# Lightning attention layer: values for four heads in 512-column matmuls, half of them passed through memory

## The chip, the cores and the metric

One core of one Trainium2 chip runs the whole kernel. The metric is the device time in microseconds (us) of one execution, median of three runs. Engines are named as in the profile: PE is the matrix engine (TensorE), PEld its weight loads, DVE the vector engine, ACT the scalar engine, POOL the GpSimd engine, SP the engine whose queue issues most transfers. A difference is stated as time after minus time before.

## The reference, cut to what matters

A decoder layer: attention over x, then a small cross attention, then a feed-forward block with 8-bit rounding. The change touches only the first part:

```python
qkv = silu(einsum('bnf,of->bno', layernorm(x), w_qkv))      # 16 heads, 128 wide, 512 inputs
q, k, v = split(qkv)                                        # per head
# per block of 64 rows: o = (q*q_decay) @ kv + (q @ k.T * diag_decay) @ v ; kv = block_decay*kv + (k*k_decay).T @ v
out = norm_w * out * rsqrt(mean(out*out) + eps)             # over all heads of a row
x = x + (sigmoid(layernorm(x) @ w_gate.T) * out) @ w_out.T
```

The input has 8 sequences of 512 rows; the kernel computes the recurrence of each head as one causal product with weights exp(-slope * distance) over the 512 rows.

## The kernel before

**Tiling.** The 16 heads are 8 pairs (p = 0 to 7). For each pair the kernel goes through the 8 sequences (b), and for each sequence through the two heads of the pair (j). One such step is a *slot*, n = 0 to 127, with v = n // 2 the number of the (pair, sequence). Every product is made of three passes over values split in a high and a low part (fp32r), listed in PASSES, so a product over 512 inputs is 4 chunks times 3 passes, 12 matmuls for a destination.

**PE in one slot**, in this order (lines of the kernel before): the scores of head n, 12 matmuls of 512, 384, 256 and 128 columns (L828); queries and keys of head n + 1, 24 matmuls of 512 columns, and the gate of head n, 12 more (all L746, `head_rows`); the output product of head n, 12 matmuls of 512 to 128 columns (L867); then half of the values of the next sequence for both heads of the pair, `values` (L755): 2 row tiles times 12 matmuls of 256 columns. In seven early slots (PREPARED) PE also transposes the normed x of a further sequence; in p = 7 it sums squares.

**DVE in one slot**: four products scores times decay, called sf (L1037 to L1041); the half of the values (product with the sigmoid, high part, low part: L890, L892, L894); the low part of the decayed scores, sl (L1049, three pieces); the same three steps for the queries and for the keys of n + 1, ending in kl; then extra work of some slots; then, when the output product is there, the gated head og (L1079), its high part (L1086) and its low part (L1088). **ACT** makes the sigmoids of values, queries, keys and gate (L614, L602, L608, L691), the high part of the scores, sh (L668), and the squares of the output, sq (L707). **POOL** adds the squares (L553), makes the low parts of weights (L453) and masks feed-forward rows (L504).

**Extra work.** From slot 29 on, feed-forward weights are prepared, one tile for every three slots: 22 tiles of 512 columns and, for the steps in slots 96 to 107, four of 1408 columns. In slots 30, 33, 36 and so on DVE finds the row scale (L979 to L986) before og, and ACT scales the rows (L621, L622) after sq. In the slots after these DVE rounds (L991, L996) before og, and ACT's queue issues a transpose (L628) after sq. ACT's sigmoid of the values comes behind these in its queue.

**Transfers.** SP loads x (2 MB, high and low, two buffers) after the gate of the second head, stores the gated heads of a sequence (1 MB, two buffers `og_out`) after og of the second head, and loads weights of the next pair, 4 times 512 KB, at the start of a pair. Everything is ordered by the loops over `slots()` and by semaphores written out by hand: an engine works off its list in order and stops at a wait.

## Time and profile before

| | |
|---|---|
| median of 3 runs | 2636.26 us (2635.76 to 2637.02) |
| profiled execution, whole | 2635.24 us |
| its span (first to last instruction) | 2633.5 us |
| PE / DVE / ACT / POOL busy | 2592.7 / 2103.1 / 1087.0 / 704.4 us |
| attention part | up to 1944.88 us, 128 slots |
| moved by transfers | 372.06 MB, mean 141 GB/s |

How to read a row of the timeline: start and length in us, engine, line, operation, destination <- sources, shape, count; in square brackets how long the engine was idle before and what ended that. The row of a matmul is longer than its distance to the next one, because matmuls overlap: what a matmul costs is the distance from start to start. The sum of 1.74 us (2635.24 less 2633.5) around the span is taken as unchanged.

### The profile page before, as it was taken

To read this page: it belongs to the slowest core of one execution; us is meant where nothing else is said; L and a number is where in the kernel's file an instruction comes from. 1 tells how busy PE (TensorE), PEld (TensorE's weight loads), DVE (VectorE), ACT (ScalarE), POOL (GpSimd) and SP (SyncE) were. 2 spreads that over 40 slices of the span, in tenths; PEclk is the share of its full clock that TensorE was granted. 3 is DMA by queue.
4 is the path that set the end of the run, shared out by engine and by line. 5 is a ranking of instruction groups with operands and counts; after the bars stand their busy time and mean duration, and the time that the engine had idled before them with its cause. 6 is when DMAs were issued, how large, how long until landed. Compare 5 with 4: busy or idle time off the path is not lost. (4 is left out here: it accounts for less than half of the span.)

```text
span 2633.5 us, 40074 instructions
## 1 busy us (share of the span) xinstructions
PE 2592.7 (98%) x14271; PEld 2174.6 (83%) x14271; DVE 2103.1 (80%) x3870; ACT 1087.0 (41%) x1848; POOL 704.4 (27%) x1034
## 2 busy tenths in 40 slices
PE   9999999999999999999999999999989999999995
PEld 8888888888888888888888888888877676767762
DVE  8887887877787788778777988776657888888887
ACT  5444322433343343334334343433224555555553
POOL 3112101311131131114111321311123444444444
PEclk9999999999999999999999999999999999999998
DMA  6653323343353334434344634342256556556642
GB/s 224 241 192 128 129 98 130 117 141 111 110 167 126 106 111 149 146 105 144 105 135 130 160 124 127 135 172 97 96 207 197 158 153 171 151 162 168 163 109 56
DMA packets 200917, 372.06 MB, mean 141 GB/s; under 512 B 97168, under 2 KB 100112, under 8 KB 192016
## 3 DMA queue, kind: packets, MB, share of 16 engines
q1 hardware_dynamic: 117024, 340.78, 38.9%
q10 hardware_dynamic: 81360, 20.07, 4.4%
q0 software_dynamic: 2336, 8.65, 1.0%
q8 instruction: 115, 1.88, 0.3%
q14 instruction: 82, 0.67, 0.1%
HBM read 252.80 MB, written 96.61 MB: 133 GB/s over the span
## 5 line engine op out<-in xcount | busy, mean ns | idle before, releaser
L746 PE MATMUL bank<-attention_xT,attention_w_hi 128*128 128x512 f32 x3064 | 952.0, 392 | 0.5 <-DVE attention_shared L947 0.5
L746 PEld LDWEIGHTS bank<-attention_xT,attention_w_hi 128*128 128x128 f32 x3064 | 566.0, 188 | 111.2 <-issue 0.6
L746 PE MATMUL bank<-attention_xT,attention_w_lo 128*128 128x512 f32 x1532 | 597.2, 390 | 0.0
L553 POOL TENSOR_TENSOR attention_sq_sum<-attention_sq_sum,attention_sq 128x512 f32<-128x512 f32 x120 | 192.1, 1601 | 1058.9 <-ACT attention_sq L707 1058.7
L755 PE MATMUL bank<-attention_w_hi,attention_xT 128*128 128x256 f32 x2048 | 379.7, 286 | 1.0 <-DMA attention_xT<-normed_turned 0.8
L746 PEld LDWEIGHTS bank<-attention_xT,attention_w_lo 128*128 128x128 f32 x1532 | 287.5, 188 | 61.7
L755 PEld LDWEIGHTS bank<-attention_w_hi,attention_xT 128*128 128x128 f32 x2048 | 317.9, 192 | 1.7 <-issue 1.7
L1037 DVE TENSOR_TENSOR attention_sf<-bank,attention_dcy 128x512 f32<-128x512 f32 (+1 forms) x256 | 147.6, 618 | 178.9 <-PE bank L828 178.7
L755 PE MATMUL bank<-attention_w_lo,attention_xT 128*128 128x256 f32 x1024 | 289.5, 283 | 0.0
L1431 PE MATMUL bank<-finish_w_out_hi,finish_og 128*128 128x512 f32 x824 | 282.4, 407 | 0.2
L668 ACT CAST attention_sh<-attention_sf 128x384 fp32r<-128x384 f32 (+1 forms) x384 | 185.4, 547 | 121.3 <-DVE attention_sf L1037 121.3
L1049 DVE TENSOR_TENSOR attention_sl<-attention_sf,attention_sh 128x384 fp32r<-128x384 f32 (+1 forms) x384 | 226.7, 645 | 0.0
L1259 POOL TENSOR_TENSOR finish_t<-finish_silu,finish_u 128x512 f32<-128x512 f32 (+1 forms) x96 | 120.3, 1253 | 309.8 <-ACT finish_silu L1329 309.8
L755 PEld LDWEIGHTS bank<-attention_w_lo,attention_xT 128*128 128x128 f32 x1024 | 196.0, 191 | 0.0
L1079 DVE SCALAR_TENSOR_TENSOR attention_og<-bank,attention_nw,attention_gate 128x512 f32<-128x512 f32 x128 | 95.9, 749 | 118.5 <-PE bank L867 118.4
L707 ACT ACTIVATE attention_sq<-bank 128x512 f32<-128x512 f32 x128 | 76.6, 599 | 273.7 <-DVE attention_og L1079 273.7
L1431 PEld LDWEIGHTS bank<-finish_w_out_hi,finish_og 128*128 128x128 f32 x824 | 154.8, 188 | 37.9 <-issue 0.4
L691 ACT ACTIVATE attention_gate<-bank 128x512 f32<-128x512 f32 x128 | 76.6, 598 | 255.4 <-PE bank L746 255.4
L608 ACT ACTIVATE attention_sig_k<-bank 128x512 f32<-128x512 f32 x128 | 76.6, 599 | 244.5 <-PE bank L746 244.5
L828 PE MATMUL bank<-attention_ql,attention_kh 128*128 128x512 f32 (+3 forms) x512 | 165.2, 323 | 0.0
L867 PE MATMUL bank<-attention_sh,attention_vl 128*128 128x512 f32 (+3 forms) x512 | 165.1, 322 | 0.0
L867 PE MATMUL bank<-attention_sl,attention_vh 128*128 128x512 f32 (+3 forms) x512 | 164.6, 321 | 0.0
(218 smaller groups left out, 4942.8 us busy)
## 6 DMA issues: line engine op xcount, KB each, us to landing
attention_xT<-normed_turned SPq DMA_DIRECT2D x62, 2048.0 KB, 8.7
gated_heads<-attention_og_out SPq DMA_DIRECT2D x64, 1024.0 KB, 7.9
finish_og<-gated_heads SPq DMA_DIRECT2D x103, 512.0 KB, 3.9
finish_og_last<-gated_heads SPq DMA_DIRECT2D x25, 512.0 KB, 4.0
normed_turned<-attention_shared SPq DMA_DIRECT2D x24, 512.0 KB, 3.9
attention_shared<-in_w_head SPq DMA_DIRECT2D x16, 512.0 KB, 8.2
finish_x<-in_x SPq DMA_DIRECT2D x32, 256.0 KB, 4.2
out<-finish_x SPq DMA_DIRECT2D x32, 256.0 KB, 4.2
```

Of the source, the lines that this page charges most:

```text
L553: g.tensor_tensor(sq_sum[:, col_b], sq_sum[:, col_b], sq[:, :], ALU.add).then_inc(s_acc, 1)
L608: nc.scalar.activation(sig_k[:, :], K_BANK[:, :], ACT.Sigmoid).then_inc(s_sigk, 1)
L668: nc.scalar.copy(sh[:, a:e], sf[:, a:e]).then_inc(s_sh, 1)
L746: mm = pe.matmul(dst[:, :], part[a][w][:, k, col:col + P], xT[i][:, b, k, :], start=(k == 0 and s == 0), stop=(k == KD - 1 and s == 2))
L755: mm = pe.matmul(bank_[:, t * 2 * P:(t + 1) * 2 * P], xT[i][:, b, k, (2 * j + t) * P:(2 * j + t + 1) * P], part[a][V_W][:, k, :], start=(k ...
L828: mm = pe.matmul(dst, (kh, kl)[a][:, t * P:(t + 1) * P], (qh, ql)[e][:, Q0[t]:S], start=(s == 0), stop=(s == 2))
L867: mm = pe.matmul(O_BANK[:, Q0[t]:S], (vh, vl)[a][i][:, t, j * P:(j + 1) * P], (sh, sl)[e][:, OFF[t]:OFF[t + 1]], start=(t == 0 and s == 0) ...
L1037: v_.tensor_tensor(sf[:, OFF[k]:OFF[k + 1]], S_BANK[k][:, 0:S - Q0[k]], d[:, 0:S - Q0[k]], ALU.mult).then_inc(s_sf, 1)
L1049: v_.tensor_tensor(sl[:, a:e], sf[:, a:e], sh[:, a:e].bitcast(F32), ALU.subtract).then_inc(s_sl, 1)
L1079: v_.scalar_tensor_tensor(out=og[:, :], in0=O_BANK[:, :], scalar=nw[:, 2 * p + j:2 * p + j + 1], in1=gate[:, :], op0=ALU.mult, op1=ALU.mul ...
L1259: g.tensor_tensor(t_[:, a:a + w], sg[k % 2][:, 0:w], u_[k % 2][:, 0:w], ALU.mult).then_inc(s_t, 1)
L1431: mm = pe.matmul(Y_BANK[:, :], og[Q % RING][:, j, a, :], wo[b][:, q * HQ + j, :], start=(q == 0 and j == 0 and s == 0), stop=(q == 3 and j ...
```

## The change

Only every other pair (even p) makes values now, for four heads at once: for one row tile, 12 matmuls of 512 columns (two pairs times two heads times 128). Such a block is called a *quad*; a sequence has four. The half for the own pair goes to the value tiles; the half for the next pair goes to a small tile `held`, is stored to memory (256 KB a quad) and is loaded again (1 MB a sequence) one pair later. `begun_in(n)` tells which two quads belong to slot n: the first is made at the end of slot n, where `values` stood, the second in slot n + 1 between the scores and the queries. Slots with v + 1 in an odd pair have none. There is one bank for both, so the second quad waits until DVE has multiplied the first by its sigmoid (semaphore `v_steps`), and DVE and ACT take the first quad at the head of slot n + 1, the second one behind sl. Before slot 0 there are three quads in place of two halves.

To make room, `og_out` and the decay table have one buffer each; the value weights (512 columns) are in one tile, refreshed in the third and seventh sequence of odd pairs; the exponentials of the decay table are made one at a time, and the triangle mask covers only 128 columns. Two more pieces of the output weights are converted ahead of slot 126.

The diff, cut to its core:

```diff
-        wh[w], wl[w] = sb(f"w_hi{w}", [P, RAW], F32R), sb(f"w_lo{w}", [P, RAW], F32R)
+    wv = [sb(f"w_{l}{V_W}", [P, KD, 4 * P], F32R) for l in ("hi", "lo")]
+    held = [sb(f"held{i}", [P, 2, 2 * P], F32R) for i in range(2)]
-    og_out[1] = sb("og_out1", [P, KT, 2, 2, P])
+    og_out = sb("og_out", [P, KT, 2, 2, P])
+    def begun_in(n):
+        v = n // 2 + 1
+        p, b = v // B, v % B
+        return None if v >= NP * B or p % 2 else KT * (p // 2 * B + b) + 2 * (n % 2)
-    SPLIT = {LAST - 13: 0, LAST - 11: 1, LAST - 9: 2, LAST - 7: 3}
+    SPLIT = {LAST - 13 + 2 * q: q for q in range(6)}
...
+            if begun_in(n - 1) is not None:
+                for q in range(2):
+                    store_values(begun_in(n - 1) + q)
+            if j == 0 and v + 1 < NP * B and (v + 1) // B % 2:
+                sp.wait_ge(s_o, n)
+                load_values((v + 1) // B, (v + 1) % B, 1 - v % 2)
...
+        values_lo(0)
+        values_lo(1)
...
         for n, v, p, b, j in slots():
-            if n < LAST:
-                sig_values(n + 1)
+            q = begun_in(n - 1)
+            if q is not None:
+                sig_values(q)
...
                 nc.scalar.copy(sh[:, a:e], sf[:, a:e]).then_inc(s_sh, 1)
+            if q is not None:
+                sig_values(q + 1)
...
+        def values(q):
+            if q > 1:
+                pe.wait_ge(s_vm, 2 * (q - 2) + 3 if q > 2 else 1)
+            for k in range(KD):
+                for s, (a, b) in enumerate(PASSES):
+                    mm = pe.matmul(v_bank(q)[:, :], xT[i][:, b, k, t * P:(t + 1) * P], wv[a][:, k, :],
+                                   start=(k == 0 and s == 0), stop=(k == KD - 1 and s == 2))
+            mm.then_inc(s_v, 1)
...
-        values(0, 0)
-        values(1, 0, v_bank(1))
+        for q in range(3):
+            values(q)
...
+            if begun_in(n - 1) is not None:
+                values(begun_in(n - 1) + 1)
             if not last:
...
-                pe.wait_ge(s_vl, n + 2)
-                values(j, 1 - i)
+            if begun_in(n) is not None:
+                wait_x(v + 1)
+                values(begun_in(n))
...
+        def values(q):
+            v_.tensor_tensor(sig_v[:, :], v_bank(q)[:, :], sig_v[:, :], ALU.mult).then_inc(s_vm, 1)
+            v_.tensor_copy(vh[i][:, t, :], sig_v[:, own])
+            v_.tensor_copy(held[r][:, 0, :], sig_v[:, other]).then_inc(s_vm, 1)
+            v_.tensor_tensor(vl[i][:, t, :], sig_v[:, own], vh[i][:, t, :].bitcast(F32), ALU.subtract)
+            v_.tensor_tensor(held[r][:, 1, :], sig_v[:, other], held[r][:, 0, :].bitcast(F32), ALU.subtract
...
             d = dcy[:, j, :]
+            q = begun_in(n - 1)
+            if q is not None:
+                values(q)
...
-            if not end:
-                values(n + 1, 1 - j, i if j == 0 else 1 - i)
...
                 v_.tensor_tensor(sl[:, a:e], sf[:, a:e], sh[:, a:e].bitcast(F32), ALU.subtract
                                  ).then_inc(s_sl, 1)
+            if q is not None:
+                values(q + 1)
...
-            if j == 0 and v >= 2:
-                v_.wait_ge(s_ogst[i], 16 * (v // 2))
+            if j == 0 and v:
+                v_.wait_ge(s_ogst, 16 * v)
```

How PE's list reads at the start of slot 66 (p = 4, third sequence), from the last scores to the first queries. Before:

```order
L828 MATMUL bank<-attention_qh,attention_kh 128x128
L828 MATMUL bank<-attention_ql,attention_kh 128x128
L828 MATMUL bank<-attention_qh,attention_kl 128x128
L746 MATMUL bank<-attention_xT_62,attention_w_hi_63 128x512 [waits attention_w2_lo_ready,attention_w2_hi_ready]
L746 MATMUL bank<-attention_xT_62,attention_w_hi_63 128x512
```

And after, where L900 are the scores, L811 the second quad and L830 the queries:

```order
L900 MATMUL bank<-attention_qh,attention_kl 128x128
L811 MATMUL bank<-attention_w_hi_53,attention_xT_62 128x512 [waits attention_v_steps,attention_w0_lo_ready,attention_w0_hi_ready]
L811 MATMUL bank<-attention_w_hi_53,attention_xT_62 128x512
L811 MATMUL bank<-attention_w_lo_54,attention_xT_62 128x512
L811 MATMUL bank<-attention_w_hi_53,attention_xT_62 128x512 x2
L811 MATMUL bank<-attention_w_lo_54,attention_xT_62 128x512
L811 MATMUL bank<-attention_w_hi_53,attention_xT_62 128x512 x2
L811 MATMUL bank<-attention_w_lo_54,attention_xT_62 128x512
L811 MATMUL bank<-attention_w_hi_53,attention_xT_62 128x512 x2
L811 MATMUL bank<-attention_w_lo_54,attention_xT_62 128x512
L830 MATMUL bank<-attention_xT_62,attention_w_hi_63 128x512 [waits attention_w2_lo_ready,attention_w2_hi_ready]
```

Twelve matmuls moved in between, with a wait for a step of DVE.

ACT's list at the change from slot 96 to slot 97 (L707/L773 squares, L621/L681 and L622/L682 scaling of a 1408-wide tile, L614/L674 sigmoid of values, L668/L732 sh, L602/L662 queries). Before:

```order
L707 ACTIVATE attention_sq<-bank 128x512
L621 ACTIVATE attention_shared<-attention_shared,attention_w_s 128x1408
L622 ACTIVATE attention_shared<-attention_shared,attention_w_s 128x1408
L614 ACTIVATE attention_sig_v<-bank 128x512
L668 CAST attention_sh<-attention_sf 128x512
L668 CAST attention_sh<-attention_sf 128x384 x2
L602 ACTIVATE attention_sig_q<-bank 128x512
```

After:

```order
L773 ACTIVATE attention_sq<-bank 128x512
L681 ACTIVATE attention_shared<-attention_shared,attention_w_s 128x1408
L682 ACTIVATE attention_shared<-attention_shared,attention_w_s 128x1408
L674 ACTIVATE attention_sig_v<-bank 128x512
L732 CAST attention_sh<-attention_sf 128x512
L732 CAST attention_sh<-attention_sf 128x384 x2
L674 ACTIVATE attention_sig_v<-bank 128x512
L662 ACTIVATE attention_sig_q<-bank 128x512
```

The first sigmoid kept its place behind the scaling, and a second one came in ahead of the queries.

## Rows read from the trace of the kernel before

**Rows 1.** The page: busy time of the engines.
```profile
PE 2592.7 (98%) x14271; PEld 2174.6 (83%) x14271; DVE 2103.1 (80%) x3870; ACT 1087.0 (41%) x1848; POOL 704.4 (27%) x1034
```

**Rows 2.** Timeline of PE, end of slot 64 and slot 65.
```profile
1006.80 0.45 PE L755 MATMUL bank<-attention_w_hi,attention_xT 128*128 128x256 f32 x2
...
1008.29 0.40 PE L755 MATMUL bank<-attention_w_hi,attention_xT 128*128 128x256 f32 x2
...
1008.65 0.40 PE L755 MATMUL bank<-attention_w_hi,attention_xT 128*128 128x256 f32 x2
...
1009.73 0.40 PE L828 MATMUL bank<-attention_qh,attention_kh 128*128 128x512 f32 x1
...
1011.58 0.67 PE L746 MATMUL bank<-attention_xT,attention_w_hi 128*128 128x512 f32 x2
...
1018.46 0.62 PE L746 MATMUL bank<-attention_xT,attention_w_hi 128*128 128x512 f32 x2
...
1019.14 0.62 PE L746 MATMUL bank<-attention_xT,attention_w_hi 128*128 128x512 f32 x2
...
1019.82 0.39 PE L867 MATMUL bank<-attention_sh,attention_vh 128*128 128x512 f32 x1
...
1021.68 0.45 PE L755 MATMUL bank<-attention_w_hi,attention_xT 128*128 128x256 f32 x2
```

**Rows 3.** Timeline of ACT, slot 65.
```profile
1009.93 0.60 ACT L614 ACTIVATE attention_sig_v<-bank 128x512 f32<-128x512 f32 x1 [1.54 <-PE bank L755]
...
1017.30 0.60 ACT L608 ACTIVATE attention_sig_k<-bank 128x512 f32<-128x512 f32 x1 [2.12 <-PE bank L746]
```

**Rows 4.** Timeline of DVE, the end of slot 64 and slot 65.
```profile
1008.25 0.69 DVE L1088 TENSOR_TENSOR attention_og_out<-attention_og,attention_og_out 128x512 fp32r<-128x512 f32 x1
...
1014.11 2.72 DVE L1049 TENSOR_TENSOR attention_sl<-attention_sf,attention_sh 128x512 fp32r<-128x512 f32 x3
...
1018.54 0.68 DVE L890 TENSOR_TENSOR attention_sig_k<-bank,attention_sig_k 128x512 f32<-128x512 f32 x1
...
1019.72 0.69 DVE L894 TENSOR_TENSOR attention_kl<-attention_sig_k,attention_kh 128x512 fp32r<-128x512 f32 x1
1021.88 0.75 DVE L1079 SCALAR_TENSOR_TENSOR attention_og<-bank,attention_nw,attention_gate 128x512 f32<-128x512 f32 x1 [1.47 <-PE bank L867]
```

**Rows 5.** Timeline of POOL, ahead of slot 0.
```profile
17.38 3.88 POOL L453 TENSOR_TENSOR attention_w_lo<-attention_shared,attention_w_hi 128x256 fp32r<-128x256 f32 x4 [13.69 <-ACT attention_w_hi L562]
23.09 2.85 POOL L453 TENSOR_TENSOR attention_w_lo<-attention_shared,attention_w_hi 128x256 fp32r<-128x256 f32 x4 [1.82 <-ACT attention_w_hi L562]
```

**Rows 6.** Timeline of PE: the queries of slot 2.
```profile
63.49 0.70 PE L746 MATMUL bank<-attention_xT,attention_w_hi 128*128 128x512 f32 x2 [0.53 <-DVE attention_shared L947]
```

**Rows 7.** Timeline of ACT, ends of slots 96 and 97 (1408-wide tiles).
```profile
1486.21 0.60 ACT L707 ACTIVATE attention_sq<-bank 128x512 f32<-128x512 f32 x1 [4.48 <-DVE attention_og L1079]
...
1489.43 0.59 ACT L614 ACTIVATE attention_sig_v<-bank 128x512 f32<-128x512 f32 x1
...
1500.93 0.60 ACT L707 ACTIVATE attention_sq<-bank 128x512 f32<-128x512 f32 x1 [4.33 <-DVE attention_og L1079]
...
1503.30 0.60 ACT L614 ACTIVATE attention_sig_v<-bank 128x512 f32<-128x512 f32 x1 [1.76 <-issue]
```

**Rows 8.** Timeline of DVE, the same slots: rounding of a 1408-wide tile, then og.
```profile
1496.96 1.62 DVE L991 SCALAR_TENSOR_TENSOR attention_shared<-attention_shared 128x1408 f32<-128x1408 bf16 x1
...
1500.15 0.74 DVE L1079 SCALAR_TENSOR_TENSOR attention_og<-bank,attention_nw,attention_gate 128x512 f32<-128x512 f32 x1
```

**Rows 9.** Timeline of PE: the first scores of slot 127.
```profile
1937.97 0.47 PE L828 MATMUL bank<-attention_qh,attention_kh 128*128 128x512 f32 x1 [2.42 <-issue]
```

**Rows 10.** Timeline of DVE, end of slot 126: kl, for which the next scores wait.
```profile
1937.17 0.69 DVE L894 TENSOR_TENSOR attention_kl<-attention_sig_k,attention_kh 128x512 fp32r<-128x512 f32 x1
```

**Rows 11.** Issues of the gated heads' store: all, and one stretch (last number: us to landing).
```profile
gated_heads<-attention_og_out SPq DMA_DIRECT2D x64, 1024.0 KB, 7.9
gated_heads<-attention_og_out SPq DMA_DIRECT2D x1, 1024.0 KB, 12.9
```

208 lines of the change are left out of this document (125 added, 83 removed).

## The prediction

> **What bounds the kernel now.** I read the page first for the busy shares: PE works 98% of the span, DVE 80% [rows 1]. Then the list of PE's waits and their places in the timeline: in the attention part the only one over 1.2 us is 2.42 us at the scores of slot 127 [rows 9]; the few others are small, as the 0.53 us of slot 2 [rows 6]. So PE's own list sets the attention part, and another engine counts only where PE comes to wait for it. Then PE's timeline of one slot [rows 2], for what a matmul costs from start to start, and ACT's and DVE's timelines of the same slot [rows 3, 4], for how close they run behind.
>
> A slot lasts from one first scores matmul to the next. In rows 2: values 2.93 us (1006.80 to 1009.73), scores 1.85 (to 1011.58), queries, keys and gate 8.24 (to 1019.82), output 1.86 (to 1021.68), and the values again; 14.87 us with values of 2.92.
>
> **Values on PE.** Three matmuls of 256 columns take 0.36 us (1008.29 to 1008.65), so one takes 0.120; three of 512 take 0.68 (1018.46 to 1019.14), so one takes 0.2267 [rows 2]. A 512-column one replaces two 256-column ones and saves 0.0133 us. A block of 24 took 2.92; a quad of 12 takes 12 x 0.2267 = 2.72. Entering a block from the 128-column matmuls costs a little: 8.24 us for 36 matmuls is 0.08 over 36 x 0.2267. So a slot with two quads (call it long) is 1.85 + 2.72 + 8.24 + 1.86 + 2.80 = 17.47, and one with none (short) is 1.85 + 0.05 + 8.24 + 1.86 = 12.00, where 0.05 is the step that the first pair after 128-column ones shows (0.67 against 0.62) [rows 2], since scores now follow the output product directly. In all there were 128 blocks x 2.92 = 373.8 us; there will be 128 x 2.72 = 348.2, plus 62 entries of 0.08 and 62 of 0.05, together 356.2. **Saving 17.6 us.** If all entries were free it would be 25.6; if every entry cost 0.13, about 9.5.
>
> **What the second quad waits for.** This is the new wait. Times from the first scores matmul of a long slot: the first quad's last matmul ends where the values' last did, so ACT's sigmoid can start at +0.20 (1009.93 against 1009.73) [rows 3], takes 0.60, and DVE's product, some 0.04 later, 0.68 like the one of the keys on the same line [rows 4]; that ends at +1.52. From a DVE end to PE's matmul I take 0.11, from kl's end at 1937.86 [rows 10] to the scores at 1937.97 [rows 9]. The quad can start at +1.63, and its turn is at +1.85. An ordinary long slot has **0.2 us of cover**, so I cost it at nothing; without cover each 0.1 us would cost 62 x 0.1 = 6.2 us. Ahead of the product on DVE stand og and its parts: og starts 0.20 after the block at the slot's end does (1021.88 less 1021.68) [rows 2, 4], its low part ends 2.14 after it (1008.94 less 1006.80), so they take 1.94 us; og may be about 1.6 us late before PE feels it. Behind the product wait everybody: PE's quad, queries, keys.
>
> **The 1408-wide tiles.** There ACT comes late. After sq starts, the scaling holds the sigmoid of the values for 3.22 us (1486.21 to 1489.43), the transpose's issue 2.37 us (1500.93 to 1503.30) [rows 7]. Let a be the start of the first quad at a slot's end. Sq starts at a + 0.98: og at a + 0.20, sq 0.78 later (1500.15 to 1500.93) [rows 7, 8]. Scaling: sigmoid at a + 4.20, product's end at a + 5.52, quad possible at a + 5.63; it is due at a + 2.80 + 1.85 = a + 4.65. PE waits **0.98 us**. Rounding: PE times the keys. Their sigmoid starts at +7.57 before (1017.30 less 1009.73) [rows 2, 3], so at +10.29 now, behind one more quad; with 0.64 for it and 1.87 for DVE's three steps (1018.54 to 1020.41) [rows 4] and 0.1 that rows overlap, DVE is free at +12.7. Rounding takes 3.19 (1496.96 to 1500.15) [rows 8], so og starts at +15.9 where the output product allows +14.87 (1021.88 less 1009.73 is 12.15 before, plus 2.72): 1.04 late. Then the quad is possible at a + 0.98 + 1.04 + 2.37 + 1.43 = a + 5.82: wait **1.17 us**. Two of the four transposes issue in about 1.4 us in place of 2.25, and cost some 0.3. All these slots, 96 to 106, are long. Sum: 4 x 0.98 + 2 x 1.17 + 2 x 0.3 = 6.9, plus about 2.2 for slot 96, which starts late because POOL's 1408-wide mask and the gate weights' low parts fall on DVE's first copies, as DVE's sl takes 2.72 us in slot 65 [rows 4], where a POOL product runs beside it, and 1.62 in quiet slots. **+9.1 us.** Bounds: 0 if ACT's queue lets the sigmoid through, 14 if each costs the wider case and the mask hits three more slots. The 512-wide tiles keep ACT busy for 1.7 us after sq; sq + 1.7 is a + 2.7 and the sigmoid is due at a + 3.0: hidden, with 0.3 us of cover.
>
> **Start.** The first quad needs high and low parts for both pairs. POOL's first low part ends at 21.26, just when PE begins its values; a second takes 2.85 to 3.88 us [rows 5], and the first may be shorter since DVE's mask is. I take **+2.7**, between 1.5 and 4. In slots 0 to 2 DVE is behind (transposes, statistics): the second quad of slot 1 and of slot 2 should wait about 1.3 and 0.8 us; in return the 0.53 us of slot 2 [rows 6] and some 1.6 us of other slack there vanish. Net 0, between -2 and +3.
>
> **Short slots.** kl is the thing to watch. Og's three steps fill DVE until +2.1, sf until +3.8, sl until +5.3, queries wait for their sigmoid and end at +7.2, keys end at about +10.0; the next scores are due at +12.0. Cover 1.9 us, against at most 1.1 us that a POOL product adds (sl 2.72 against 1.62). Nothing, except slot 28, where scores wait for name sums: +0.3. Refresh and decay table in the slots around a change of pair: +0.6.
>
> **One buffer for gated heads.** The store is issued about +2.2 into the next slot, and DVE writes the buffer again after that slot's og, at +12.95 in a short slot: 10.8 us. It lands in 7.9 us at the median, 12.9 with a transpose beside it [rows 11]. The late ones make DVE wait up to 2.1 us, which the cover of kl in the following slot takes. Cost 0.3. The added traffic is 128 stores of 256 KB and 32 loads of 1 MB; behind their waits on SP's queue stand only transfers with a slot of room.
>
> **End.** In slots 126 and 127 no values were made. The 2.42 us wait [rows 9] is scores of slot 127 waiting for kl, which ended at 1937.86 [rows 10] because POOL converted three pieces of output weights beside DVE. Two of the three move ahead into slots with cover. I expect that wait gone, and 1.2 of it back as a wait of the last output product for sl: **-1.2**.
>
> **Sum**: -17.6 + 9.1 + 2.7 + 0 + 0.3 + 0.6 + 0.3 - 1.2 = -5.8. The profiled execution's 2635.24 (1.0 below the median) gives 2629.4; against the median of 2636.26 it is **2630.5 us**.
>
> **Rivals.** (A) The sum as it stands: half of its spread (2625 to 2636) lies under 2631.0. Chance 0.53. (B) The waits of the 1408-wide tiles don't appear, or nearly: -5.8 - 9.1 = -14.9, 2621.4. For it: the sigmoid waits only for PE in most rows. Against it: ACT's list has no way around L621 and L622 [rows 7]. Chance 0.15. (C) Slower: the second quad waits in every long slot, since its cover of 0.2 us is a difference of rows. It decides from a lateness of 0.2 us; at 0.45 us late it costs 62 x 0.25 = 15.5, giving 2646. For it: og's low part or a POOL product can push DVE; against: og had waited 1.47 us for PE [rows 4], and with its 1.94 us it is over at 1023.82, before the next scores at 1024.60. Chance 0.13. (D) The store of the gated heads lands late in many short slots, for the value load and the x load share its queue: at 12.9 us in each of the 31 pairs of short slots, 2.1 late, of which a third passes the cover: 31 x 0.7 = 21.7 at worst, some 8 if a third of them do, 2638. For it: the 12.9; against: the queue is in order and the store goes ahead of the value load. Chance 0.14. (E) The change saves PE less than its rows say. Rows 2 give a fixed 13.4 ns beside 512 columns at 2.4 GHz (226.7 less 213.3) and the same 13.3 at 256, so two shapes agree. Were a fixed part of 2.5 ns all that is saved, it would be 1536 x 0.0025 = 3.8 in place of 20.5, and the whole 2647. Chance 0.03. The Trainium skill (TensorE: Matmul & The Clock Gate, "Wait — 56ns, not 53.3ns?") puts matmuls at columns over 2.4 GHz plus about 2.5 ns; it measured other operands, and the trace disagrees. The last 0.02 is for mishaps.
>
> **How the numbers follow.** The predicted time is A's, 2630.5. The range 2619 to 2643 holds A, B and the milder ends of C and D. A measurement can tell about 0.2%, 5.3 us: faster means below 2631.0, slower above 2641.5. Faster: half of A and all of B with a little of D, 0.45; slower: most of C, a part of D, E and the tail of A, 0.17; same 0.38.
>
> **What would show it.** In the timeline after: long slots of 17.47 us and short ones of 12.00; the second quad starting 1.85 after the scores with no idle time; idle time of about 1 us ahead of it in slots 97, 98, 100, 101, 103, 104, 106 and 107, ended by DVE's product; PE idle near 21.3 for about 2.7 us; no wait at the scores of slot 127. Idle time in ordinary long slots would be C, idle time ahead of scores in short ones, behind DVE's gated head waiting for a store, would be D.

## The result, and the profile after

| | us |
|---|---|
| kernel before, median of 16 runs | 2636.16 (2634.46 to 2637.34) |
| changed kernel, median of 16 runs | 2643.33 (2639.22 to 2647.32) |
| ratio, 95% interval | 1.0027 (1.0020 to 1.0034) |
| profiled execution before: time, span | 2635.24, 2633.5 |
| profiled execution after: time, span | 2639.46, 2637.7 |

The change made the kernel slower, by 7.2 us of median; the forecast was 2630.5, with a range that ended at 2643.0. The profiled execution of the changed kernel lies 3.9 us below its median, so it shows less than a typical one lost; a second trace of the same kernel (below) is needed for the rest.

The page after. Against [rows 1] PE issues 1536 matmuls fewer and is busy 12.8 us less, in a span that is 4.2 us longer:

```profile
PE 2579.9 (98%) x12735; PEld 2101.0 (80%) x12735; DVE 2127.5 (81%) x4126; ACT 1100.4 (42%) x1862; POOL 694.2 (26%) x1034
```

PE's timeline around slot 108, an ordinary long slot, is the counterpart of [rows 2] (start, duration, engine, line; L900 scores, L811 values, L830 queries, keys and gate, L946 output). The first scores are at 1689.37 and 1706.81, so the slot lasts 17.44 us. The second quad starts 1.86 after the scores, with no idle time, and the quads take 2.78:

```profile
1686.59 0.68 PE L811 MATMUL bank<-attention_w_hi,attention_xT 128*128 128x512 f32 x2
...
1689.37 0.39 PE L900 MATMUL bank<-attention_qh,attention_kh 128*128 128x512 f32 x1
...
1691.23 0.68 PE L811 MATMUL bank<-attention_w_hi,attention_xT 128*128 128x512 f32 x2
...
1694.01 0.62 PE L830 MATMUL bank<-attention_xT,attention_w_hi 128*128 128x512 f32 x2
...
1706.81 0.39 PE L900 MATMUL bank<-attention_qh,attention_kh 128*128 128x512 f32 x1
```

PE's list of waits after (engine, line, what ended the wait: us in all, times, longest). The first line is new, and is the main place where time was lost; the second tells of DVE; the line of L1520 stands for a wait of 6.4 us before:

```profile
PE bank L811 <- DVE attention_sig_v L980: 13.1, 12, 3.4
...
DVE attention_og_out L1173 <- DMA gated_heads<-attention_og_out: 10.5, 6, 3.7
...
PE bank L1520 <- DVE finish_x L1633: 7.6, 1, 7.6
...
PE bank L811 <- POOL attention_w_lo L506: 2.4, 1, 2.4
...
PE bank L946 <- issue: 1.9, 1, 1.9
```

**The 1408-wide tiles.** Slots 97 to 107 last 205.33 us, and eleven ordinary long slots would last 191.84: 13.5 us more. 5.1 of them are in slot 97. PE's timeline there, with the counterpart of the second quad above:

```profile
1481.25 0.68 PE L811 MATMUL bank<-attention_w_hi,attention_xT 128*128 128x512 f32 x2
...
1484.04 0.39 PE L900 MATMUL bank<-attention_qh,attention_kh 128*128 128x512 f32 x1
...
1489.50 1.19 PE L811 MATMUL bank<-attention_w_hi,attention_xT 128*128 128x512 f32 x2 [3.45 <-DVE attention_sig_v L980]
...
1493.75 0.62 PE L830 MATMUL bank<-attention_xT,attention_w_hi 128*128 128x512 f32 x2
```

DVE first computes a row maximum of 1.61 us ahead of og; ACT then squares, scales twice (1.46 each) and only then takes the sigmoid of the quad that PE finished at 1484.04; the product at 1488.66 frees the bank. These are ACT's and DVE's timelines, the counterparts of [rows 7, 8]:

```profile
1484.77 0.60 ACT L773 ACTIVATE attention_sq<-bank 128x512 f32<-128x512 f32 x1 [3.34 <-DVE attention_og L1166]
1485.26 1.46 ACT L681 ACTIVATE attention_shared<-attention_shared,attention_w_s 128x1408 bf16<-128x1408 f32 x1
1486.62 1.46 ACT L682 ACTIVATE attention_shared<-attention_shared,attention_w_s 128x1408 f32<-128x1408 f32 x1
1487.98 0.58 ACT L674 ACTIVATE attention_sig_v<-bank 128x512 f32<-128x512 f32 x1
```

```profile
1481.84 1.61 DVE L1061 TENSOR_REDUCE attention_w_s<-attention_shared 128x1 f32<-128x1408 f32 x1
...
1483.98 0.75 DVE L1166 SCALAR_TENSOR_TENSOR attention_og<-bank,attention_nw,attention_gate 128x512 f32<-128x512 f32 x1
...
1488.66 0.69 DVE L980 TENSOR_TENSOR attention_sig_v<-bank,attention_sig_v 128x512 f32<-128x512 f32 x1 [1.47 <-ACT attention_sig_v L674]
```

After the 3.45 us of idle time the quad took 4.25 us (1489.50 to 1493.75) instead of 2.78. The stretches' table shows a lower clock (length, busy us of PE, PEld, DVE, ACT and POOL with counts, granted clock of PE as a share of full speed, DMA share, GB/s): the granted clock was 0.64 in those 4.2 us.

```profile
1489.50:1493.70 4.20, 4.20 (x12) 3.38 (x13) 4.17 (x11) 1.45 (x3) 0.00 (x0) 0.64 0.18 62
```

The rest of the 13.5 us is in the slots behind scaling (1.14 each in slots 100, 103 and 106), in those behind rounding (1.42, 0.48, 1.52 and 0.49 in slots 98, 101, 104 and 107), and in slot 99 (1.09). The last has a cause of its own: POOL's mask of a 1408-wide tile ran beside DVE's copy of the gated head at the end of slot 98, which took 2.26 us where such copies take 0.43, so that the first quad's product came late (DVE's and POOL's timelines):

```profile
1523.61 2.26 DVE L1173 CAST attention_og_out<-attention_og 128x512 fp32r<-128x512 f32 x1
```

```profile
1522.71 2.87 POOL L558 TENSOR_TENSOR attention_shared<-attention_shared,down_named 128x1408 f32<-128x1408 f32 x1 [14.07 <-DMA attention_shared<-in_f_down]
```

**Start.** The first quad waits for POOL's second low part. It should be read with [rows 5]:

```profile
23.82 0.70 PE L811 MATMUL bank<-attention_w_hi,attention_xT 128*128 128x512 f32 x2 [2.41 <-POOL attention_w_lo L506]
```

```profile
17.39 2.90 POOL L506 TENSOR_TENSOR attention_w_lo<-attention_shared,attention_w_hi 128x256 fp32r<-128x256 f32 x4 [14.30 <-ACT attention_w_hi L624]
20.25 3.42 POOL L506 TENSOR_TENSOR attention_w_lo<-attention_sq_sum,attention_w_hi 128x256 fp32r<-128x256 f32 x4
```

The three quads then took 9.85 us (23.82 to the scores of slot 0 at 33.67) at a granted clock of 0.83, and slots 0 to 2 last 61.49 us. In each of them the second quad waits for DVE's product: 0.73, 0.98 and 1.24 us.

**Short slots** last 12.00. Some are longer much as they were before (slots 27, 28 and those in p = 7 that sum squares); new are the excesses of slots 48, 55 and 61, of 0.23, 0.63 and 0.56. That of slot 48 isn't a store's: it stands in the run with a store for each head too (0.21). In slot 61 DVE's copy of the gated head waited for the store of the pair before:

```profile
954.32 0.43 DVE L1173 CAST attention_og_out<-attention_og 128x512 fp32r<-128x512 f32 x1 [2.70 <-DMA gated_heads<-attention_og_out]
```

The store's median landing hardly moved, 8.0 us against 7.9 in [rows 11].

**End.** The wait at the scores of slot 127 [rows 9] is gone, and the last output product waits instead. Slots 126 and 127 up to the finishing part are 0.8 us shorter. But the finishing part, from the first matmul with the output weights to the end, takes 691.7 us where it took 688.6. Its first wait grew from 6.37 to 7.63 us, and one for a transposed transfer from 0.38 to 1.85:

```profile
1944.04 0.47 PE L946 MATMUL bank<-attention_sh,attention_vh 128*128 128x512 f32 x1 [1.87 <-issue]
...
1965.69 0.76 PE L1520 MATMUL bank<-finish_w_out_hi,finish_og_last 128*128 128x512 f32 x1 [7.63 <-DVE finish_x L1633]
```

### The profile page after: what moved, and what is told of

Read it like the earlier page. It is cut to its first block, busy times and chain, and to the rows that moved or that the text cites. A ratio compares the mean times of both kernels' runs of the same rounds, so it can differ in the third digit from the quotient of the medians.

```text
span 2637.7 us, 37691 instructions
## 1 busy us (share of the span) xinstructions
PE 2579.9 (98%) x12735; PEld 2101.0 (80%) x12735; DVE 2127.5 (81%) x4126; ACT 1100.4 (42%) x1862; POOL 694.2 (26%) x1034
## 4 chain that ended last, share of the span: by engine, by line
PE 92%; DVE 4%; ACT 1%; issue 1%; DMA 1%; POOL 0%; ACTq 0%; SPq 0%; DVEq 0%; POOLq 0%
PE bank L830 39%; PE bank L1520 13%; PE bank L811 12%; PE bank L946 8%; PE bank L900 8%; PE bank L1564 6%; PE bank L1574 3%; PE bank L1541 1%; PE bank L1530 1%; DVE attention_sig_v L980 0%; DVE attention_og L1166 0%; DMA finish_qT<-finish_q 0%; PE bank L838 0%; DMA finish_tT<-down_named 0%; PE bank L1552 0%
## 5 line engine op out<-in xcount | busy, mean ns | idle before, releaser
L830 PE MATMUL bank<-attention_xT,attention_w_hi 128*128 128x512 f32 x3064 | 947.1, 390 | 0.0
L830 PEld LDWEIGHTS bank<-attention_xT,attention_w_hi 128*128 128x128 f32 x3064 | 570.4, 188 | 114.9
L830 PE MATMUL bank<-attention_xT,attention_w_lo 128*128 128x512 f32 x1532 | 596.2, 389 | 0.0
L811 PE MATMUL bank<-attention_w_hi,attention_xT 128*128 128x512 f32 x1024 | 325.8, 400 | 15.7 <-DVE attention_sig_v L980 13.1
L830 PEld LDWEIGHTS bank<-attention_xT,attention_w_lo 128*128 128x128 f32 x1532 | 287.5, 188 | 59.9
L732 ACT CAST attention_sh<-attention_sf 128x384 fp32r<-128x384 f32 (+1 forms) x384 | 186.0, 547 | 285.4 <-DVE attention_sf L1124 285.2
L1520 PE MATMUL bank<-finish_w_out_hi,finish_og 128*128 128x512 f32 x824 | 282.5, 407 | 0.2
L811 PEld LDWEIGHTS bank<-attention_w_hi,attention_xT 128*128 128x128 f32 x1024 | 184.6, 190 | 49.8 <-issue 17.5
L811 PE MATMUL bank<-attention_w_lo,attention_xT 128*128 128x512 f32 x512 | 201.0, 393 | 0.0
L1520 PEld LDWEIGHTS bank<-finish_w_out_hi,finish_og 128*128 128x128 f32 x824 | 154.8, 188 | 37.9 <-issue 0.4
L668 ACT ACTIVATE attention_sig_k<-bank 128x512 f32<-128x512 f32 x128 | 76.6, 598 | 241.0 <-PE bank L830 241.0
L773 ACT ACTIVATE attention_sq<-bank 128x512 f32<-128x512 f32 x128 | 76.5, 598 | 232.7 <-DVE attention_og L1166 232.7
L900 PE MATMUL bank<-attention_qh,attention_kl 128*128 128x512 f32 (+3 forms) x512 | 165.3, 323 | 0.0
L946 PE MATMUL bank<-attention_sh,attention_vl 128*128 128x512 f32 (+3 forms) x512 | 165.1, 322 | 0.0
L900 PE MATMUL bank<-attention_ql,attention_kh 128*128 128x512 f32 (+3 forms) x512 | 164.8, 322 | 0.0
L946 PE MATMUL bank<-attention_sl,attention_vh 128*128 128x512 f32 (+3 forms) x512 | 164.6, 321 | 0.0
L900 PE MATMUL bank<-attention_qh,attention_kh 128*128 128x512 f32 (+3 forms) x512 | 161.3, 315 | 1.1 <-issue 0.9
```

The costliest lines, as they stand in the source:

```text
L732: nc.scalar.copy(sh[:, a:e], sf[:, a:e]).then_inc(s_sh, 1)
L811: mm = pe.matmul(v_bank(q)[:, :], xT[i][:, b, k, t * P:(t + 1) * P], wv[a][:, k, :], start=(k == 0 and s == 0), stop=(k == KD - 1 and s == 2))
L830: mm = pe.matmul(dst[:, :], part[a][w][:, k, col:col + P], xT[i][:, b, k, :], start=(k == 0 and s == 0), stop=(k == KD - 1 and s == 2))
L900: mm = pe.matmul(dst, (kh, kl)[a][:, t * P:(t + 1) * P], (qh, ql)[e][:, Q0[t]:S], start=(s == 0), stop=(s == 2))
L946: mm = pe.matmul(O_BANK[:, Q0[t]:S], (vh, vl)[a][i][:, t, j * P:(j + 1) * P], (sh, sl)[e][:, OFF[t]:OFF[t + 1]], start=(t == 0 and s == 0) ...
L1520: mm = pe.matmul(Y_BANK[:, :], og[Q % RING][:, j, a, :], wo[b][:, q * HQ + j, :], start=(q == 0 and j == 0 and s == 0), stop=(q == 3 and j ...
```

## Experiments

The theory after the first trace: the values cost PE what the prediction says, and the saving of 17.6 us is spent mostly on the **second quad**, which finds its bank still unread (theory Q), on its aftermath in the granted clock (theory C), and on **stores that land late** in short slots (theory D). Later a fourth came up, the mask of POOL beside DVE (theory P). "The changed kernel" has two sets of runs, with medians of 2643.33 us and, in a later set, 2640.41; a gain against it is therefore given as a range. The medians of the kernel before were 2635.55, 2636.02 and 2636.08 us in the three sets of runs. Where a span is given, it is that of the profiled execution.

### Tiles of 1408 in short slots

```diff
-    tasks = [(kind, t) for t in range(KF) for kind in "gu"] + [("d", t) for t in range(KD)]
+    tasks = [(kind, t) for t in range(KF) for kind in "gu"]
+    tasks[6:6] = [("d", t) for t in range(KD)]
```

> The changed kernel with one edit: the four down-projection row tiles, 1408 elements wide, take places 6 to 9 in the list of tiles instead of the last four, so that they are scaled in slots 48, 51, 54 and 57, which have no quads of values; nothing is left out. Theory Q (the second quad of a slot waits for the product of the first, and that product stands behind the 1408-wide work on ACT and DVE): in the profile of the changed kernel slots 97 to 107 were 13.4 us longer than eleven times 17.44; that goes, the 1408-wide work in short slots costs under 1.5 us, and the time is 2643.3 - 12 = 2631 us. Rival W (the 1408-wide work costs its time wherever it stands, through contention for on-chip memory or the DMA queue): slots 48 to 58 grow by 8 to 13 us in return and the time stays within 2 us of 2643.

Measured: 2644.17 us (2642.98 to 2645.11, 7 runs), ratio 1.0032 (1.0020 to 1.0043). Theory Q was right about the place that was left: slots 97 to 107 last 17.44 each, 13.5 us less. Rival W was right about the place that was entered: slots 48 to 61 went from 169.5 to 187.1 us. Short slots have no quad whose bank can be late; they have only 12 us, in which DVE, with 3 us of rounding more, splits the next keys too late, so that the next scores wait. 7.6 of the 17.6 us are in slot 57 alone, where also a transposed transfer and the gated heads' store landed late together (timelines of DVE, ACT and PE):

```profile
918.50 0.43 DVE L1174 CAST attention_og_out<-attention_og 128x512 fp32r<-128x512 f32 x1 [8.17 <-DMA gated_heads<-attention_og_out]
```

```profile
916.78 3.33 ACT L699 ACTIVATE attention_x_in<-attention_shared,cnt_col 128x128 f16<-128x128 bf16 x11 [8.46 <-DMA attention_shared<-attention_x_in]
```

```profile
925.42 0.76 PE L947 MATMUL bank<-attention_sh,attention_vh 128*128 128x512 f32 x1 [5.73 <-DVE attention_sl L1135]
```

So neither of the two places tried is free for the 1408-wide work; what can be moved is who waits behind it.

### ACT's scaling behind the first sigmoid

```diff
             if q is not None:
                 sig_values(q)
+            if n - 1 in SCALED:
+                scaled(SCALED[n - 1])
+            if n - 1 in ROUNDED:
+                turn_weights(ROUNDED[n - 1])
...
-            if n in SCALED:
-                scaled(SCALED[n])
-            if n in ROUNDED:
-                turn_weights(ROUNDED[n])
```

> The changed kernel with one edit: ACT's two scaling activations, and its issue of the transposing transfer, move from the end of a slot to the next slot, behind the sigmoid of the first quad and ahead of the copies of the scores, where ACT was idle for 2.81 us in slot 108; nothing is left out. Theory Q-ACT (most of the waits of second quads are ACT's queue): the scaling slots lose their 1 us each and slot 97 most of its 5.07 us, the rounding slots (97, 100, 103, 106, in which DVE's og is 1.04 us late) keep a part; of the 13.4 us in slots 97 to 107 between 6 and 10 go, and the time is about 2635. Rival Q-DVE (the lateness is DVE's: the row maximum of 1.61 us and the two rounding operations ahead of og): under 4 us go, the time is 2640 or more. Either way the two activations may now hold up the copies of the scores; if they do, og is late in scaling slots everywhere and short slots show it.

Measured: 2632.44 us (2627.49 to 2636.38, 11 runs), ratio 0.9987 (0.9978 to 0.9996): 11 us under the changed kernel in its first set of runs, 8 under its second. In the trace slots 97 to 107 hold 7.7 us over 191.84, 5.8 less than before the edit. Slots 98, 100, 101, 103, 104, 106 and 107 now last 17.43 to 17.45, the rounding slots as well, since the transpose's issue had moved too. The wait of slot 97 fell from 3.45 to 2.01, what is left being DVE's lateness. Slots 99 and 105 have waits of 1.70 and 1.74 us. In 99 DVE's copy of the gated head took 3.09 us in place of 0.43 (more on such copies below). In 105 ACT copied the transposed tile so late that its square and the sigmoid behind it came late: issuing the transpose a little later costs there. Theory Q-ACT had forecast 6 to 10 us and about 2635, its rival under 4 us. The sum, 5.8, lies between them because of the two longer waits in slots 99 and 105; of the waits in the other slots 8.6 of 12.4 us went, so the greater part of those was ACT's queue. The median fell by more than the 4.4 us of the span, which these traces don't explain.

### A store for each head

```diff
-                sp.wait_ge(s_ogl, 2 * n + 2)
-                sp.dma_start(og_dram[b, p].rearrange("t e f -> e t f"),
-                             og_out[:, :, :, :, :].rearrange("p t j l c -> p t (j l c)")
-                             ).then_inc(s_ogst, 16)
+            sp.wait_ge(s_ogl, 2 * n + 2)
+            sp.dma_start(og_dram[b, p].rearrange("t e f -> e t f")[:, :, j * 2 * P:(j + 1) * 2 * P],
+                         og_out[:, :, j, :, :].rearrange("p t l c -> p t (l c)")
+                         ).then_inc(s_ogst[j], 16)
...
-            if j == 0 and v:
-                v_.wait_ge(s_ogst, 16 * v)
+            if v:
+                v_.wait_ge(s_ogst[j], OGST[j] + 16 * v)
```

> The changed kernel with one edit: the gated heads are stored one head at a time, each at the end of its own slot, with a semaphore for each half of the buffer, so that a half is needed again two slots after its store instead of one; nothing is left out. Theory D (DVE's copy of the gated head waits for the store of the pair before: 2.70 us in slot 61, less in 48 and 55): these waits go and 1.4 us with them in the profiled execution, and if they are what makes the executions of the changed kernel spread over 8 us (2639 to 2647) where those of the kernel before lie within 3, the median falls by 3 to 5 us and the spread to 3. Rival: the store is only one of many transfers that share the queue, the median stays within 1.5 us of 2643 and the spread stays.

Measured: 2634.79 us, ratio 0.9998 (0.9989 to 1.0007); ten of the 11 runs lie between 2633.14 and 2635.75, one at 2642.33. No wait of DVE for a store is left in the list. The span fell by 4.0: slots 48 to 61 last 168.24 (169.46 before), and the finishing part takes 689.5 instead of 691.7. Half of the last store now goes 8 us earlier; whether that is what shortens the finishing part isn't shown, as it took 688.7 in one run below with the store undivided. Theory D holds in sign and place: the edit is worth 5.6 to 8.5 us of median, of which the trace has 1.2 in slots 48 to 61 and 2.3 in the finishing part. The rest is argued from the longer waits that other traces of the changed kernel show (below).

### The values' transfers cut to one partition

```diff
-            sp.dma_start(dram.v[b, :, :, t, :], held[r][:, :, :].bitcast(F32)).then_inc(s_held[r], 16)
+            sp.dma_start(dram.v[b, 0:1, :, t, :], held[r][0:1, :, :].bitcast(F32)).then_inc(s_held[r], 16)
...
-                sp.dma_start(dst[:, :, :].rearrange("p t c -> p (t c)").bitcast(F32),
-                             dram.v[b, :, l].rearrange("p t c -> p (t c)")).then_inc(s_vld[i], 16)
+                sp.dma_start(dst[0:1, 0, :].bitcast(F32), dram.v[b, 0:1, l, 0, :]).then_inc(s_vld[i], 16)
```

> The changed kernel with the values' transfers cut to one partition (a store of 2 KB and loads of 1 KB, in place of 256 KB and 128 partitions of 4 KB), all waits and all other work kept; the values of odd pairs are therefore not those of the kernel, and only the transfers' volume is left out. Theory T (the extra traffic delays the gated heads' store and the finishing part's loads, and makes the spread): the late stores of slots 48, 55 and 61 go, the finishing part falls back from 691.7 to 688.6 us, and the median is 2637 to 2640 with a spread of 3 us. Rival N (volume does not matter, 166 GB/s is far from full): within 1.5 us of 2643.

Measured: 2638.06 us (2636.07 to 2640.39, 11 runs), ratio 1.0009 (1.0000 to 1.0018). The volume of the detour through memory is worth 2 to 5 us of median. Whether by way of the late stores isn't shown: DVE's waits for them halve, here from 10.5 to

```profile
DVE attention_og_out L1172 <- DMA gated_heads<-attention_og_out: 5.4, 7, 1.6
```

and slots 48 to 61 last 168.26 us, but one trace of a kernel with the full volume (dummy matmuls, below) has 6.0 and 168.32. The spread was 4.3 us, not 3. The finishing part did not follow (691.6 us), so that half of theory T is wrong.

### The second quad between queries and keys

```diff
-            if begun_in(n - 1) is not None:
-                values(begun_in(n - 1) + 1)
...
                 head_rows(Q_BANK, w, 0, i2).then_inc(s_q, 1)
+                if begun_in(n - 1) is not None:
+                    values(begun_in(n - 1) + 1)
                 head_rows(K_BANK, w, P, i2).then_inc(s_k, 1)
```

On ACT the second sigmoid, and on DVE the second product, move the same way between those of the queries and of the keys.

> The changed kernel with one edit: the second quad of a slot stands between the matmuls of the next queries and those of the next keys instead of ahead of both, and its sigmoid and product move with it on ACT and DVE; nothing is left out. In the changed kernel the product of the first quad has 1.85 us (the scores) to be done in; here it has 1.85 + 2.7 us, and the next first quad is 7 us away. Theory Q (the second quad waits for the bank): slots 97 to 107 all last 17.44 us (13.4 us less in sum), slots 0 to 2 lose some 2 of their 3.9 us over 57.6, and the time is 2643.3 - 15 = 2628 us. Rival R (the wait only moves: the same product and splits now delay the keys' split, so that the next scores wait for kl): the long slots with 1408-wide work wait at the scores, under 6 us are won and the time is 2637 or more.

Measured: 2626.26 us (2624.18 to 2628.23, 5 runs), ratio 0.9961 (0.9947 to 0.9975), so 17 us under the changed kernel (14 under its second set). Slots 97 to 107 sum to 192.05: of the 13.5 us 13.3 are gone, while the same work stands on the same engines. PE's timeline of slot 97, the counterpart of the 3.45-us wait above: scores, queries, second quad and keys follow each other without idle time.

```profile
1484.88 0.39 PE L900 MATMUL bank<-attention_qh,attention_kh 128*128 128x512 f32 x1
...
1486.73 0.68 PE L830 MATMUL bank<-attention_xT,attention_w_hi 128*128 128x512 f32 x2
...
1489.52 0.63 PE L811 MATMUL bank<-attention_w_hi,attention_xT 128*128 128x512 f32 x2
...
1492.29 0.61 PE L830 MATMUL bank<-attention_xT,attention_w_hi 128*128 128x512 f32 x2
```

This settles Q. R holds only for slot 96, 0.9 us longer. The span fell by 11.2 us; that the median fell by 14 to 17 isn't explained by this one trace. The expectation for slots 0 to 2 was wrong: they got 0.9 us longer. The second quad had stood ahead of slot 2's queries while DVE finished the last split of the next rows; without it PE waits for that split:

```profile
77.12 0.70 PE L830 MATMUL bank<-attention_xT,attention_w_hi 128*128 128x512 f32 x2 [1.76 <-DVE attention_shared L1029]
```

### The kernel before with one buffer

```diff
-            if j == 0 and v >= 2:
-                v_.wait_ge(s_ogst[i], 16 * (v // 2))
-            hi, lo = og_out[i][:, :, j, 0, :], og_out[i][:, :, j, 1, :]
+            if j == 0 and v:
+                v_.wait_ge(s_ogst[1 - i], 16 * ((v + 1) // 2))
+            hi, lo = og_out[0][:, :, j, 0, :], og_out[0][:, :, j, 1, :]
```

SP's store reads the same buffer.

> The kernel before with one part of the change alone: one buffer for the gated heads, so that the copy of a pair's first head waits for the store of the pair before it; nothing is left out. Theory D (late stores are what put the median of the changed kernel 4 us above its profiled execution and spread it over 8 us): here too the median rises by 2 to 6 us, to 2638 to 2642, the executions spread over more than 4 us, and the trace shows DVE's copy waiting for the store in some slots. Rival: the store is late only behind the values' transfers, which the kernel before does not have; then the time stays within 1 us of 2635.6.

Measured: 2635.32 us (2633.54 to 2637.41, 11 runs), ratio 0.9997 (0.9988 to 1.0006). DVE does wait for stores here, up to 2.9 us at a time:

```profile
DVE attention_og_out L1086 <- DMA gated_heads<-attention_og_out: 6.2, 3, 2.9
```

but these waits are in slots 2, 97 and 105, none in slots 48 to 61, and no slot up to 126 is longer for them. So the single buffer costs nothing by itself in slots of 14.87 us. In the changed kernel it stands beside slots of 12.00 us and the traffic of the values; no run parts the two.

### Dummy matmuls in two idle stretches

```diff
+        keep_warm(40)
         for q in range(3):
             values(q)
...
+            if n == 97:
+                keep_warm(56, Q_BANK)
             if begun_in(n - 1) is not None:
                 values(begun_in(n - 1) + 1)
```

> The changed kernel with dummy matmuls of 128 columns in two idle stretches of TensorE: 40 ahead of the first quad, where it waited 2.41 us for POOL, and 56 into the queries' bank ahead of the second quad of slot 97, where it waited 3.45 us for DVE; nothing is left out. Theory C (the idle itself costs as much again through the granted clock: the second quad of slot 97 took 4.25 us in place of 2.82, and the three first quads 9.85 us in place of 8.5): the quad of slot 97 takes 2.8 us, the three first ones 8.5 us, and the scores of slot 0 start 1.3 us earlier. Rival: the quads are slower for another reason (weights or operands still being written), their times stay, and the dummy matmuls win nothing.

Measured once: 2634.67 us, span 2632.9. PE's timeline in slot 97, and the table of the quad's stretch:

```profile
1483.87 3.30 PE L824 MATMUL bank<-attention_ones 128*128 128x128 f16 x56
...
1487.47 0.70 PE L811 MATMUL bank<-attention_w_hi,attention_xT 128*128 128x512 f32 x2 [0.30 <-DVE attention_sig_v L983]
...
1490.31 0.61 PE L830 MATMUL bank<-attention_xT,attention_w_hi 128*128 128x512 f32 x2
```

```profile
1487.47:1490.31 2.84, 2.84 (x12) 2.33 (x13) 2.81 (x9) 0.97 (x3) 0.00 (x0) 1.00 0.15 52
```

The granted clock is 1.00 instead of 0.64, and the quad takes 2.84 us instead of 4.25. At the start the three quads take 8.29 us (23.80 to 32.09) instead of 9.85. In slot 97 C holds: six traces of the same place without dummy matmuls have waits of 2.0 to 3.45 us and then quads of 4.25 to 5.26 us, this one has neither. At the start it doesn't follow from this run. The run with earlier transfers (below) has the start as in the changed kernel, with its wait of 2.41 us and no dummy matmuls, and its clock stayed at 1.00 too, with 8.27 us for the three quads:

```profile
23.68:31.95 8.27, 8.27 (x37) 6.84 (x37) 7.01 (x15) 2.13 (x3) 7.64 (x16) 1.00 0.11 37
```

In the seven other traces with that wait (2.36 to 2.43 us) the three quads took 9.7 to 9.9 us, at 0.83 or 0.84. So the lower clock costs some 1.5 us there when it comes, and what the dummy matmuls did about it is open. Of the gain at the start 0.8 us was given back at once, in slot 0 (21.26 for 20.47), and slots 97 to 107 together are no shorter than without the edit (205.62 for 205.33): slots 99 and 105 are longer by 0.6 and 0.9 us, as in this trace POOL's mask ran beside DVE's copies of the gated head ahead of them (2.88 and 2.03 us). The rest of the distance to the changed kernel's span isn't these edits': 3.1 us lie in the finishing part (688.7) and 1.1 in slots 48 to 61.

### The changed kernel again

> The changed kernel once more, unaltered, for a second trace of it: its profiled execution (2639.5 us) lay 4 us under the median of its executions (2643.3, spread over 8 us), while storing each head by itself brought the median down by 8.5 us but the profiled span by 4 only. Theory D (stores of gated heads that land late): a typical execution has one or more slots in which DVE's copy of the gated head waits 4 us or more for the store, as the run with the 1408-wide tiles in short slots had once, 8.17 us in its slot 57. Theory P (POOL's mask of a 1408-wide tile, 2.87 us, stretches whichever DVE operation runs beside it from 0.69 to 3.3 us, and where it falls depends on when the rows land): the difference stands in slots 97 to 107, which then hold more than the 13.4 us over 17.44 each that the first trace showed. Rival: the trace repeats the first one to 1 us and the spread is in the finishing part.

Measured: 2640.41 us (2637.34 to 2644.08, 11 runs), ratio 1.0017 (1.0008 to 1.0026); span 2641.3, so 3.6 more than the first trace. Up to slot 47 the two agree to 0.05 us. Slots 48 to 63 last 204.52 us instead of 201.79. In slot 61 DVE waited longer still for the store, and PE waited 1.75 us at the scores of slot 62, where it had been 0.39 (timelines of DVE and PE):

```profile
955.05 0.43 DVE L1173 CAST attention_og_out<-attention_og 128x512 fp32r<-128x512 f32 x1 [3.58 <-DMA gated_heads<-attention_og_out]
```

```profile
964.44 0.47 PE L900 MATMUL bank<-attention_qh,attention_kh 128*128 128x512 f32 x1 [1.75 <-issue]
```

Slot 62 itself then lasts 16.44 us instead of 14.82, without any further wait: the granted clock behind the wait was 0.66. The stretches' table for its first 4.56 us:

```profile
964.44:969.00 4.56, 4.56 (x17) 3.98 (x18) 4.46 (x9) 1.02 (x2) 1.81 (x2) 0.66 0.92 326
```

Slots 97 to 107 sum to 205.58, as in the first trace (205.33), but not slot by slot. Slot 97 is 1.4 us longer: behind the same wait of 3.45 us the quad took 5.26, at a granted clock of 0.50. Slot 99 is 1.1 shorter: POOL's mask stretched DVE's copy to 1.09 us only, for 2.26. So the difference between the traces is D's and, behind a wait, the clock's (C), and P's works the other way; 0.6 us more are in the finishing part. A third trace, that of the next run, which leaves these slots as they are, has waits of 4.21 and 4.28 us for the store and 172.0 us in slots 48 to 61. The single executions fit: the three of the 16 with a mean granted clock of 0.992 or 0.993 took 2639.5 to 2640.9 us, the five at 0.989 or 0.990 took 2643.1 to 2647.3. That late stores alone make the spread isn't shown: the run with the 1408-wide tiles in short slots has the longest wait for one, 8.17 us, and spread over 2.1 us only.

### Earlier transfers for the finishing part

```diff
-            if n == LAST - 1:
-                sp.wait_ge(s_g, n)
+            if n == LAST - 2:
+                sp.wait_ge(s_g, n + 1)
                 for Q in range(early.RING - 1):
                     load_heads(sp, Q)
+            if n == LAST - 1:
...
```

> The changed kernel with one edit: the four transfers of gated heads for the finishing part are issued at the end of the gate's matmuls of slot 125, ahead of the last store but one, instead of behind it; nothing is left out. Theory F (the finishing part starts by transfers; in the changed kernel its last slots are 3.1 us shorter and these transfers were issued 18.95 us ahead of its first matmul in place of 22.64, so that what the attention part won at its end was given back): the stretch from the first matmul with the output weights to the end, 691.7 us against 688.6 before, falls to 688 to 689, and the time by some 3 us to 2640. Rival: these four transfers are not what is late there (the mask and the context rows, queued behind the last store, are), and the stretch stays at 691.5 or more.

Measured: 2642.37 us (2640.16 to 2644.64, 10 runs), ratio 1.0021 (1.0011 to 1.0030). The transfers were issued 24.6 us ahead of the first matmul with the output weights, and the finishing part took 692.9 us: theory F is wrong. The three quads at the start took 8.27 us, as told above.

### Four edits together

The second quad later, a store for each head, the earlier transfers, and for the very first quad the products of the weights' low part last, behind the eight others:

```diff
+            order = [(k, s) for k in range(KD) for s in range(3)]
+            if q == 0:
+                order.sort(key=lambda ks: ks[1] == 2)
+            for k, s in order:
+                if q == 0 and (k, s) == (0, 2):
+                    pe.wait_ge(s_wl[V_W], v // B + 2)
...
```

> The changed kernel with four edits at four places: the second quad later (as in the run of that name), a store for each head (as in the run of that name), the very first quad with its products of the low part of the weights last, so that POOL's 2.41 us are covered by eight matmuls, and the four transfers of gated heads for the finishing part ahead of the last store but one instead of behind it; nothing is left out. If the waits are as the traces say, the terms add: 2643.3 - 15 (second quads) - 8.5 (stores) - 1.8 (first quad) - 1 (earlier transfers at the end) = 2617 us. If two of them share a cause, the sum falls short: over 2621. If the first quad's part fails, the scores of slot 0 stand at 33.3 us as before and not at 31.7.

Measured: 2626.47 us (2624.44 to 2627.90, 5 runs), ratio 0.9963 (0.9949 to 0.9976): no better than the second quad's move alone. The parts did what they should: scores of slot 0 at 30.51 us (33.71 in the run with the later second quad alone), a finishing part of 687.9 (691.6). Against them stand two of slot 0's microseconds (22.47 for 20.43, the next rows not yet split) and new time in slots 98 (21.54 us) and 104 (18.74). In slot 98 PE waited 2.23 us for the last quad's low part, which stood on DVE behind a subtraction of 3.29 us; others of its kind take 0.69. POOL's mask of a 1408-wide tile ran beside it (timelines of DVE, POOL and PE):

```profile
1510.53 3.29 DVE L974 TENSOR_TENSOR attention_ql<-attention_sig_q,attention_qh 128x512 fp32r<-128x512 f32 x1
```

```profile
1510.39 2.87 POOL L560 TENSOR_TENSOR attention_shared<-attention_shared,down_named 128x1408 f32<-128x1408 f32 x1 [6.12 <-DMA attention_shared<-in_f_down]
```

```profile
1515.80 0.50 PE L954 MATMUL bank<-attention_sh,attention_vh 128*128 128x512 f32 x1 [2.23 <-DVE attention_held L997]
```

The next first quad took 3.98 us for 2.8, at a granted clock of 0.69. The subtraction starts 0.14 us after the mask and ends at 1513.82, 0.56 after it: an operation of 0.69 us, it seems to have done nearly all its work once POOL was done. The Trainium skill (SBUF — State Buffer, "Who interferes with whom") says that a DVE instruction with two inputs in SBUF contends with a GpSimd instruction that reads SBUF, and that the later one blocks until the other ends; this trace agrees, with 3.29 us for 0.69.

### All waits

To these four edits come two: in slot 2 the second quad keeps its old place, and POOL's mask waits for the split of the next keys.

```diff
             g.wait_ge(s_rows, 16 * n + 16)
+            if tasks[n][0] == "d":
+                g.wait_ge(s_kl, FIRST + STEP * n + 2)
...
```

> The four edits of the run e7 and two more: in slot 2 the second quad stays ahead of the queries (there it covered the last split of the next rows, for which TensorE waited 1.77 us in e7), and POOL's mask of the four 1408-wide tiles waits until the next keys are split, so that it falls into DVE's idle time ahead of the gated head; nothing is left out. Theory P: the 3.29-us subtraction in slot 98 becomes 0.7, slots 98 and 104 (21.54 and 18.74 us) fall to 17.44, slot 2 from 22.81 to about 20.6, and the time is 2626.5 - 5.4 - 2 = 2619 us. Rival: the mask now stretches the operations of the gated head (og, its copy and its remainder), which makes ACT's sigmoid and the first quad's product late; then slots 96, 99, 102 and 105 wait in return and the time stays over 2623.

Measured: 2622.66 us (2620.76 to 2624.46, 5 runs), ratio 0.9946 (0.9932 to 0.9959). Slots 98 and 104 last 17.47 and 17.44, as theory P has it, and the same subtraction takes 0.69. The mask now stretches the copy of the gated head, and the addition of squares, which POOL starts behind it at 1517.11, the remainder (DVE's and POOL's timelines). That was the rival, but none of slots 99, 102 and 105 is longer; only slot 96 lasts 18.41, as in the run before:

```profile
1509.67 0.69 DVE L980 TENSOR_TENSOR attention_ql<-attention_sig_q,attention_qh 128x512 fp32r<-128x512 f32 x1
...
1515.39 2.03 DVE L1189 CAST attention_og_out<-attention_og 128x512 fp32r<-128x512 f32 x1
1517.45 1.66 DVE L1191 TENSOR_TENSOR attention_og_out<-attention_og,attention_og_out 128x512 fp32r<-128x512 f32 x1
```

```profile
1514.24 2.89 POOL L562 TENSOR_TENSOR attention_shared<-attention_shared,down_named 128x1408 f32<-128x1408 f32 x1 [10.86 <-DVE attention_kl L980]
```

Slot 2 gave 1.0 us, not 2.2, and the finishing part took 1.7 us more than in the run before (689.6), so the time is 3.7 over the expected 2619. It beats both kernels: 13.4 us under the kernel before. The change was worth making; it needed another order around it. What the edits that don't touch the quads (the store for each head, the earlier transfers, the mask's place) would give the kernel before wasn't tried.

## Why the prediction was wrong, step by step

The forecast for the profiled execution was 2629.4, and 2639.46 was measured. Its sum said 5.8 us faster, and the traces say 4.2 us slower. The terms that failed are the cost of the 1408-wide tiles (13.5 us for 9.1), the finishing part, which was put at nothing without a reason (+3.1), slots 0 to 2 (+1.7 for 0), the start (+4.0 for 2.7) and the single buffer for gated heads (1.7 for 0.3, and 4.4 in the second trace). What was missing in three of them is the same: the lower clock behind a wait of PE. By its own steps:

- **Values on PE**: right. Long slots last 17.44 (17.47 forecast), short ones 12.00 (12.00). Fifty-nine long slots at 0.03 less make -1.8. Rival E is out.
- **Cover of the second quad in ordinary long slots**: right; no idle time there, and rival C is out. The cover was as thin as it said, though, which is why everything late on ACT or DVE became a wait.
- **The 1408-wide tiles**: right mechanism, size short, 13.5 for 9.1. The waits are in the slots it named, and in the one of slot 97 3.45 us stand for the 0.98 + 2.2 forecast. Three things were missing. The granted clock after the idle time costs 1.4 us in slot 97. The waits behind scaling cost 1.14 for 0.98 and those behind rounding 1.42, 1.52, 0.48 and 0.49 for 1.17 and 0.3. And slot 99 had 1.09, from the mask beside DVE's copy; the prediction counted the mask for slot 96 alone. Moving the quad took away 13.3 of the 13.5, moving ACT's work 5.8. Rival B is out.
- **Start**: the wait for POOL was 2.41, forecast 2.7. The term came out at 4.0, as the clock behind that wait was not counted; in the run with earlier transfers the clock stayed up, and the term was 2.3.
- **Slots 0 to 2**: forecast 0 net, measured +1.7. The waits of 0.98 and 1.24 us for the product were expected (1.3 and 0.8), the one of 0.73 in slot 0 wasn't. With the 0.53 gone that would be +2.4, so that of the 1.6 us of slack that were to vanish in return only 0.7 did.
- **One buffer for gated heads**: the prediction gave 0.3 us and had the store's landing, 7.9 to 12.9 us against 10.8, in front of it, so DVE would wait 2.1 us at most, and the 1.9 us of cover of kl would take that. DVE waited up to 3.7 us in the first trace and 4.3 in the third. Slots 48 to 63 hold 1.7 us over their 200.1 in the first trace (0.2 of it in slot 48, not the store's) and 4.4 in the second, where the clock behind the wait makes 1.6 of it; and the store for each head brought the median down by 5.6 to 8.5. Rival D was thus partly true, beside A instead of in its place. The kernel before, with one buffer, has three waits of DVE of the kind and no longer slot.
- **Refresh, slot 28, decay table**: forecast 0.3 + 0.6, found 0.4 in slots 27 and 28 and 0.3 in slot 12, whose cause isn't known.
- **End**: -0.8 for -1.2.
- **The finishing part**: not in the prediction, +3.1. It took 688.6 and 686.5 us in the two traces of kernels with the old values, which don't differ there, and 691.6 to 692.9 in seven of those with the new ones, but 688.7 with the dummy matmuls and 687.9 to 689.6 in the three with a store for each head. Issuing four transfers earlier or leaving out the values' volume changed nothing. In the first trace the first wait (+1.3) and the one for a transposed transfer (+1.5) make nearly all of it. The first ends with the context rows' landing. Why they land about a microsecond later, and why the transposed transfer does, stays open.

Together: 2629.4 - 1.8 (values) + 4.4 (tiles) + 1.3 (start) + 1.7 (slots 0 to 2) + 1.4 (slots 48 to 63, 1.7 less the 0.3 forecast) - 0.2 (refresh) + 0.4 (end) + 3.1 (finishing part) = 2639.7, against 2639.46. The step from there to the median of 2643.3 is likely the late stores and the clock behind waits: the second trace, 3.6 us longer, has 2.7 of them in slots 48 to 63 and 1.4 in slot 97, less 1.1 in slot 99. The error of method: each wait was priced by the idle time that it makes, and neither the clock after it (3.0 us in the first trace and 5.6 in the second, against the same matmuls at 1.00) nor its variation between executions was priced at all.

## What to carry to other kernels

A change that saves time on the busiest engine also shortens the time in which the others must be done; whatever was covered by the old slot (a store behind one buffer, 3 us of rounding on DVE) has to be costed against the new one. When two blocks of the same bank follow each other with 0.2 us of cover, move the second one behind other matmuls: here one reordering was worth 14 to 17 us, nearly as much as the saving of PE that the change was made of. A wait of the matrix engine can cost nearly as much again in the lower clock behind it: here 1.4 to 2.4 us behind waits of 1.75 to 3.45, in some executions and not in others. And sums of gains measured one at a time hold only until the next thing queued on the shared engine is late, so look at the trace of the combination.

## What the runs showed of the hardware

- After 3.45 us without matmuls PE's granted clock was 0.64 over the next 4.2 us, a mix of the 1.2 and 2.4 GHz levels, and the 12 matmuls of 512 columns took 4.25 us; with dummy matmuls of 128 columns in the gap it was 1.00 and they took 2.84. In two other traces the same gap was followed by 0.50 and 5.26 us (the second trace and the run with earlier transfers).
- The length of the gap alone does not decide. After 2.41 us the clock was 0.83 over the next 9.85 us in the first trace, and 1.00 over the same matmuls, 8.27 us, in the run with earlier transfers; after 1.75 us, at the scores of slot 62 in the second trace, it was 0.66 over the next 4.56 us.
- A subtraction of DVE with both inputs in SBUF took 3.29 us beside a product of POOL of 2.87 us, and 0.69 alone; a copy of 512 elements took 2.03 and 2.26 for 0.43.
- A store of 1 MB of gated heads lands in 8 us at the median, and yet DVE waited for one 8.17 us in slot 57 of one run, where a transposed transfer was late as well.
- The same kernel, with 2640.41 and 2643.33 us as medians of two sets of runs, differs by more than the kernel before in four sets (2635.55 to 2636.16). Its waits differ between traces in length (for the store of slot 61: 2.70, 3.58 and 4.28 us) and in the clock behind them.
